# The convolution's bias goes into X ahead of time, and relu and sum become one VectorE operation

## The chip, the cores and the metric

The kernel runs on one core of a Trainium2 chip. The metric is the time of one execution on the device, in microseconds (us). The engines are named as in the profile: PE is TensorE (PEld its weight loads), ACT is ScalarE, DVE is VectorE, POOL is GpSimd, SP issues the DMAs.

## What is computed

For 32 images of 64 channels and 32 x 32 positions: a group norm, a convolution block, an attention block and a layer of eight experts with a residual around each. Only the first block matters here.

```python
def _L0_conv_ref(x, info_w, info_b, mask_w, mask_b, out_w, out_b):
    info = relu(einsum('ic,bchw->bihw', info_w, x) + info_b)
    mask = sigmoid(einsum('mc,bchw->bmhw', mask_w, x) + mask_b)
    expanded = (mask[:, :, None] * info[:, None]).reshape(B, MC * IC, H, W)
    return relu(einsum('oe,behw->bohw', out_w, expanded) + out_b)
...
x = x + _L0_conv_ref(_gn(x), ...)
t = tokens(x)
t = t + attention(_ln_t(t), ...)
t = t + experts(_ln_t(t), ...)
```

Everything is in float32. Since relu(z + b) = max(z, -b) + b, the sum x + relu(z + b) equals max(z, -b) + (x + b).

## The kernel before

Two images lie on the 128 partitions (a pair), with 1024 positions each. A group is two pairs (slots s = 0 and 1, `G = 2`), and there are eight groups. Each slot is worked on in two halves c of 512 columns. So a step over "pieces" is four instructions, (s, c) = (0,0), (0,1), (1,0), (1,1).

The work of a group is cut into stages with names. In one turn, group a goes through its dense stages (norm, convolution, attention) while the group before it goes through the experts: 32 units of 128x1024 hidden values, taken in 16 batches of two. A step marked H does the first layers and the Gelus of a batch (PE L794, ACT L942); a step marked Y does its second layers, the weighting and the sum (PE L809, DVE L1277, POOL L988). The table `SCHEDULE` says in which order the stages and the H and Y steps stand, the same for all engines, and each engine works through its own part of it strictly in that order. The first turn has a table of its own, `OPENING`: there group 1 (`EARLY`) is worked on beside group 0, with other buffers (XF for X, CWB for T1 and the rest, the banks HP for R).

The stages that the change touches:

- `group_norm`: DVE subtracts the mean and multiplies (L1082, 128x1024, one for each slot), from X to XN, and signals `gn_done`. Then PE multiplies XN for `info_mask_0` and `info_mask_1` (L557), ACT does relu and tanh of the result in T1 (L859, L860), and DVE splits that into two parts (L1089, L1091). `SCHEDULE` has a Y step between `group_norm` and `info_mask_0`, and an H, Y, H behind `info_mask_0`.
- `conv_out`: PE multiplies by the weights "ow" into the banks R (L587). ACT reads R, scales by 0.5, adds the bias, does relu, writes T1 and signals `oc_act` (L871). DVE adds T1 to X in place and signals `x1_done` (L1106).
- `centre_1`: PE multiplies the new X by a centering matrix into the same banks R (L642, behind `x1_done`), ACT squares (L876), DVE sums the squares (L1127). Then `rstd_1`, a chain of short DVE operations.
- `features_1` copies results of the norm to XN and XB on ACT (L884, L887), and POOL adds X to XB (L978).
- `choose_1` and `choose_2` are the DVE operations that pick two experts for each token (L1212 to L1252).
- `prepare`: some DVE operations on weights at the start, once.

Of the kernel before, what the change touches and what calls it, by code (L numbers as in the profile page):

```python
# [11 lines left out]
ALU = mybir.AluOpType  # L12
# [3 lines left out]
P = 128  # L16
# [4 lines left out]
G = 2  # L21
# [89 lines left out]
def build(nc, x, wpack, w1e, reps, out):  # L111
    xd = x.rearrange("(n two) c t -> n (two c) t", two=2)
    od = out.rearrange("(n two) c t -> n (two c) t", two=2)
    with ExitStack() as ctx:
        def sb(name, shape, dt=F32):
            return ctx.enter_context(nc.sbuf_tensor(name, shape, dt))

        def sem(name):
            return ctx.enter_context(nc.semaphore(name))

        def sems(name):
            return [sem(f"{name}{g}") for g in range(G)]
# [25 lines left out]
        W1G = sb("W1G", [P, HID])  # L148
        BH = sb("BH", [P, 1])
        BT = sb("BT", [P, 1])  # L150
        ONE = sb("ONE", [P, 2], BF16)
        MINUS = sb("MINUS", [P, 1])
        BI = sb("BI", [P, 2, 2])
# [14 lines left out]
        def w(name, rows=slice(0, P)):  # L168
            a, n = COLS[name]
            return W[rows, a:a + n]  # L170

        def col(k, rows=slice(0, P)):
            a = COLS["cols"][0] + k
            return W[rows, a:a + 1]
# [6 lines left out]
        def half(c):  # L181
            return slice(c * CH, (c + 1) * CH)
# [51 lines left out]
        ir_done = sems("ir_done")  # L234
        prod_done = sems("prod_done")
        oc_ps = sems("oc_ps")
        oc_act = sems("oc_act")
        x1_done = sems("x1_done")
        ln_ps = sems("ln_ps")
        ln_sq = sems("ln_sq")  # L240
# [60 lines left out]
        def pieces(slots):  # L301
            return [(s, c) for s in slots for c in range(NCH)]
# [4 lines left out]
        def nth(n, s, c=None):  # L307


            if c is None:  # L310
                return (n - 1) * G + s + 1
            return ((n - 1) * G + s) * NCH + c + 1

        def at(n, c):

            return (n - 1) * NCH + c + 1
# [36 lines left out]
        def slotwise(name, stage):  # L353

            return {f"{name}.{s}": (lambda s=s: stage((s,))) for s in range(G)}
# [51 lines left out]
        def convolution_buffers(a):  # L407

            if a == EARLY:
                return XF[:, 1, :, :], CWB[:, :, 0, :], CWB[:, :, 1, :], CWB[:, :, 2, :], CWB[:, :, 3:7, :], HP  # L410
            return X, XN, T1, T2, BIG, R
# [117 lines left out]
        def _(pe):  # L529
# [11 lines left out]
            def parts(a, b, par):  # L541
# [208 lines left out]
                def gates():  # L750

                    for s in range(G):
                        pe.wait_ge(xf_done[s], at(a + 1, LAST))
                        if a == 0:
                            pe.wait_ge(oc_act[s], at(EARLY + 1, LAST))
                    for part in range(2):
                        for s in range(G):
                            for h in range(2):
                                strip = 32 * (2 * s + h)
                                tokens_4 = XF[:, par, s, :].rearrange("p (q r t) -> p r q t", r=4, t=P)[:, 2 * h + part, :, :]  # L760
                                last = mm(Rg[0][strip:strip + 32, 0:T // 4], GWZ[:, 2 * E * (1 - part):2 * E * (3 - part)], tokens_4,
                                          start=(part == 0), stop=(part == 1))
                    last.then_inc(gate_ps, 1)
# [77 lines left out]
        def _(act):  # L841
# [10 lines left out]
            def parts(a, b, par):  # L852
                Xa, XNa, T1a, T2a, BIGa, Ra = convolution_buffers(a)

                def info_mask(s):

                    act.wait_ge(im_ps, nth(a + 1, s))
                    info, mask = img(s), img(1 - s)
                    f(T1a[info, s, 0:CH], Ra[s][info, 0:CH], ACT.Relu, bias=BI[info, 0, 0:1])  # L859
                    f(T1a[mask, s, 0:CH], Ra[s][mask, 0:CH], ACT.Tanh, bias=BT[mask, :], scale=0.5).then_inc(im_act, 1)  # L860

# [2 lines left out]
                        act.wait_ge(rep_ps[s], at(a * NREP + 3 * k + 1, c))  # L864
                        f(T2a[:, s, half(c)], Ra[s][:, half(c)], ACT.Copy).then_inc(ir_done[s], 1)

                def conv_out(slots):

                    for s, c in pieces(slots):
                        act.wait_ge(oc_ps[s], at(a + 1, c))  # L870
                        f(T1a[:, s, half(c)], Ra[s][:, half(c)], ACT.Relu, bias=col(B_OUT), scale=0.5).then_inc(oc_act[s], 1)  # L871

                def square(k, slots):
                    for s, c in pieces(slots):
                        act.wait_ge(ln_ps[s], at(a * LNS + k, c))
                        f(T2[:, s, half(c)], R[s][:, half(c)], ACT.Square).then_inc(ln_sq[s], 1)  # L876
# [23 lines left out]
                def copy_out(ready, n, dst, done, slots):  # L900
                    for s, c in pieces(slots):
                        act.wait_ge(ready[s], at(n, c))
                        f(dst[:, s, half(c)], R[s][:, half(c)], ACT.Copy).then_inc(done[s], 1)

                def exponential(n, slots):
                    for s, c in pieces(slots):
# [38 lines left out]
                def expert(step, m):  # L945
# [1 line left out]
                        gelus(m)  # L947

                return {
                    "info_mask_0": lambda: info_mask(0), "info_mask_1": lambda: info_mask(1),  # L950
                    **slotwise("info_0", lambda slots: info(0, slots)), **slotwise("info_1", lambda slots: info(1, slots)),
                    **slotwise("conv_out", conv_out), **slotwise("centre_1", lambda slots: square(1, slots)),
                    **slotwise("features_1", features_1), **slotwise("query", lambda slots: exponential(1, slots)),
                    **slotwise("key", lambda slots: exponential(2, slots)), **slotwise("kv_turn", kv_turn),
                    **slotwise("numerator", numerator), **slotwise("message", lambda slots: square(2, slots)),
# [43 lines left out]
        def _(dve):  # L999
# [3 lines left out]
            def prepare():  # L1003

                dve.wait_ge(w_rest, 16)
                v.tensor_scalar(W1G[:, :], w("w1"), col(G1), None, ALU.mult).then_inc(dve_prep, 1)
                dve.wait_ge(prep_pe, 1)
                v.tensor_copy(WMC[:, :], YP[0][:, 0:P]).then_inc(dve_prep, 1)
                v.tensor_copy(W2C[:, :], YP[0][:, P:P + C]).then_inc(dve_prep, 1)
                v.tensor_copy(BH[:, :], YP[0][:, P + C:P + C + 1]).then_inc(dve_prep, 1)  # L1010
                v.memset(GWZ[:, :], 0.0).then_inc(dve_prep, 1)
                dve.wait_ge(dve_prep, 5)
                dve.wait_ge(pads_set, 1)
                v.tensor_copy(GWZ[:, 2 * E:4 * E], w("gw")).then_inc(dve_prep, 1)
                dve.wait_ge(dve_prep, 6)
                v.memset(ST[:, 0, 30:31], 0.0).then_inc(prep_done, 1)

            def parts(a, b, par):
# [66 lines left out]
                def info_mask(s):  # L1085

                    dve.wait_ge(im_act, nth(a + 1, s))
                    high = IM[:, s, 0, :]
                    v.tensor_copy(high, T1a[:, s, 0:CH]).then_inc(hl_high, 1)  # L1089
                    dve.wait_ge(hl_high, nth(a + 1, s))  # L1090
                    v.tensor_tensor(IM[:, s, 1, :], T1a[:, s, 0:CH], high.bitcast(F32), ALU.subtract).then_inc(hl_done, 1)  # L1091
# [10 lines left out]

                def conv_out(slots):
                    for s, c in pieces(slots):
                        dve.wait_ge(oc_act[s], at(a + 1, c))
                        v.tensor_tensor(Xa[:, s, half(c)], Xa[:, s, half(c)], T1a[:, s, half(c)], ALU.add)\  # L1106
                            .then_inc(x1_done[s], 1)
                        if c == LAST and a != EARLY:
                            set_ones(s)
# [277 lines left out]
```

## Time and profile before

| what | value |
|---|---|
| median of 3 runs | 1195.16 us (1192.1 to 1196.35) |
| the profiled execution, its own time | 1201.06 us |
| its span in the trace | 1199.2 us |
| PE busy | 1075.0 us, 90% |
| DVE busy | 783.8 us, 65% |
| ACT busy | 681.4 us, 57% |
| POOL busy | 359.3 us, 30% |

The profile is of one execution. The chain that ended last, followed back from the last instruction, lies for 68% of the span on PE, 16% on DVE and 12% on ACT. A steady turn takes about 141 us, and it repeats nearly to the hundredth of a microsecond: L1082 starts at 542.22 us in one turn, and the ACT operation behind it (L859) at 262.38, 403.30, 544.22, 685.14, 826.06 and 967.01 us in the six turns that have it. All numbers of one place are therefore given for the turn around 542 us. A figure such as "x2 2.12" is the time from the start of the first of two instructions to the end of the second.

### The profile page before, as it was taken

How to read it: one execution, taken by the hardware profiler on the slowest of the kernel's cores; microseconds unless marked ns; L12 is line 12 of the kernel's file. 1: busy time of each engine (PE TensorE's matmuls, PEld its weight loads, DVE VectorE, ACT ScalarE, POOL GpSimd, SP SyncE). 2: the span in 40 equal slices, each digit the busy share in tenths (PEclk: the TensorE clock that was granted, in tenths of full speed). 3: DMA queues.
4: the chain of work that ended last, by engine and by line, in shares of the span. 5: the costliest groups of instructions: out<-in, count | busy, mean ns of one | idle time of the engine just before them, and what ended most of it. 6: DMA issues, size and time to landing. Idle time of an engine off the chain costs nothing.

```text
span 1199.2 us, 15483 instructions
## 1 busy us (share of the span) xinstructions
PE 1075.0 (90%) x5863; PEld 497.3 (41%) x5878; DVE 783.8 (65%) x1673; ACT 681.4 (57%) x930; POOL 359.3 (30%) x277
## 2 busy tenths in 40 slices
PE   5888759989999899998999989998999989999898
PEld 2454526433554245442453424542354424534232
DVE  4764746588556975488655886659754887547434
ACT  2336345755755656665657656565566555676454
POOL 0100031244312433134322344123431342314465
PEclk9987889999999999999999999999999999999999
DMA  4010069006810095102940059100771019400580
GB/s 148 1 36 1 1 145 211 1 18 132 207 36 18 1 210 129 34 18 53 223 98 1 18 119 219 36 15 4 166 173 36 19 29 222 88 1 18 113 198 27
DMA packets 17418, 96.64 MB, mean 81 GB/s; under 512 B 3648, under 2 KB 6720, under 8 KB 13120
## 3 DMA queue, kind: packets, MB, share of 16 engines
q1 hardware_dynamic: 17344, 95.66, 34.5%
q8 instruction: 46, 0.75, 0.3%
q14 instruction: 28, 0.23, 0.1%
HBM read 77.82 MB, written 9.44 MB: 73 GB/s over the span
## 4 chain that ended last, share of the span: by engine, by line
PE 68%; DVE 16%; ACT 12%; issue 3%; SPq 1%; DMA 0%; DVEq 0%; POOL 0%; POOLq 0%; ACTq 0%
PE HP L809 14%; PE HP L794 12%; PE R L642 7%; PE R L729 5%; ACT H L942 5%; PE R L598 5%; PE R L587 4%; PE R L578 3%; DVE SM L1127 3%; PE R L660 3%; PE R L651 2%; PE R L736 2%; PE R L809 2%; DVE TM L1277 2%; ACT XB L887 1%
## 5 line engine op out<-in xcount | busy, mean ns | idle before, releaser
L988 POOL TENSOR_TENSOR XB<-TM,XB 128x512 f32<-128x512 f32 x254 | 321.3, 1287 | 670.4 <-DVE TM L1277 670.3
L942 ACT ACTIVATE H<-HP,W 128x1024 f32<-128x1024 f32 x224 | 237.6, 1113 | 112.3 <-PE HP L794 111.8
L794 PE MATMUL HP<-XF,W1E 64*128 64x512 f32 x1024 | 256.0, 618 | 24.3 <-DVE TM L1277 23.8
L1277 DVE SCALAR_TENSOR_TENSOR TM<-HP,B2S,CWB 128x512 f32<-128x512 f32 x224 | 161.5, 746 | 132.4 <-PE HP L809 129.1
L809 PE MATMUL HP<-H,W 128*64 128x512 f32 x896 | 226.4, 613 | 22.1 <-ACT H L942 22.1
L794 PEld LDWEIGHTS HP<-XF,W1E 64*128 64x128 f32 x1024 | 87.3, 185 | 148.1 <-DVE TM L1277 82.2
L876 ACT ACTIVATE T<-R 128x512 f32<-128x512 f32 x128 | 73.8, 598 | 101.5 <-PE R L642 89.0
L809 PEld LDWEIGHTS HP<-H,W 128*64 128x64 f32 x896 | 49.4, 135 | 170.6 <-ACT H L942 132.5
L1127 DVE TENSOR_REDUCE SM<-T 128x8 f32<-128x512 f32 x128 | 85.1, 684 | 29.5 <-ACT T L876 27.3
L1099 DVE SCALAR_TENSOR_TENSOR BIG<-R,T 128x512 f32<-128x512 f32 x112 | 70.2, 685 | 30.1 <-PE R L578 29.8
L598 PE MATMUL R<-W,T 128*128 128x128 f32 x512 | 73.4, 289 | 5.7 <-DVE T L1146 5.2
L1154 DVE SCALAR_TENSOR_TENSOR BIG<-T,R 128x512 f32<-128x512 f32 x64 | 41.8, 684 | 49.7 <-ACT T L908 49.7
L598 PEld LDWEIGHTS R<-W,T 128*128 128x128 f32 x512 | 56.8, 145 | 40.5 <-DVE T L1146 33.7
L729 PE MATMUL R<-BIG,W1G 128*128 128x512 f32 x128 | 64.5, 633 | 2.2 <-ACT BIG L894 0.5
L1146 DVE TENSOR_TENSOR T<-R,SM 128x512 f32<-128x512 f32 x96 | 59.6, 683 | 0.6
L908 ACT ACTIVATE T<-R,MINUS 128x512 f32<-128x512 f32 x64 | 41.4, 687 | 19.7 <-PE R L651 19.6
L587 PE MATMUL R<-BIG,W 128*64 128x512 f32 x224 | 52.6, 623 | 0.0
L578 PE MATMUL R<-IM,REP 32*128 32x512 f32 x336 | 49.4, 475 | 2.9 <-DVE IM L1091 1.6
L978 POOL TENSOR_TENSOR XB<-XB,X 128x1024 f32<-128x1024 f32 x14 | 32.9, 2354 | 61.3 <-ACT XB L887 61.3
L871 ACT ACTIVATE T<-R,W 128x512 f32<-128x512 f32 x28 | 19.2, 687 | 53.8 <-PE R L587 53.8
L1277 DVE SCALAR_TENSOR_TENSOR TM<-R,B2S,CWB 128x512 f32<-128x512 f32 x32 | 23.9, 751 | 37.9 <-PE R L809 32.0
L942 ACT ACTIVATE BIG<-HP,W 128x1024 f32<-128x1024 f32 x32 | 33.9, 1110 | 26.0 <-PE HP L794 26.0
(165 smaller groups left out, 1363.9 us busy)
## 6 DMA issues: line engine op xcount, KB each, us to landing
CWB<-gates_hbm SPq DMA_DIRECT2D x32, 1536.0 KB, 22.0
CWB<-gates_hbm SPq DMA_DIRECT2D x32, 512.0 KB, 10.0
BIG<-XN SPq DMA_DIRECT2D x32, 256.0 KB, 4.5
out<-XB SPq DMA_DIRECT2D x15, 512.0 KB, 2.9
X<-x SPq DMA_DIRECT2D x14, 512.0 KB, 7.8
W<-wpack SPq DMA_DIRECT2D x1, 1064.0 KB, 5.0
XF<-x SPq DMA_DIRECT2D x2, 512.0 KB, 6.2
gates_hbm<-CWR SPq DMA_DIRECT2D x16, 64.0 KB, 1.6
```

The source lines that it names most:

```text
L578: last = mm(Ra[s][:, half(c)], REP[rows, n, :], IM[rows, s, part, :], start=(part == 0), stop=(part == 1))
L587: last = mm(Ra[s][img(k), half(c)], w("ow")[:, C * h:C * h + C], BIGa[:, s, 2 * k + h, half(c)], start=(h == 0), stop=(h == 1))
L598: last = nc.tensor.transpose(R[s][:, P * j:P * j + P], src[:, s, P * j:P * j + P], w("ident"))
L642: last = mm(R[s][:, P * j:P * j + P], src[:, s, P * j:P * j + P], weights, start=True, stop=True)
L729: mm(R[s][:, half(c)], W1G[:, :], U[s][k][:, half(c)], start=True, stop=True)\
L794: last = mm(HP[u % BATCH][:, half(k)], W1E[img(k), e, :], XF[img(k), 1 - par, s, half(c)], start=True, stop=True)
L809: last = mm(sums_of(b, u)[img(k), :], w("w2e")[:, C * e:C * e + C], activated(b, u)[:, k, :], start=True, stop=True)
L876: f(T2[:, s, half(c)], R[s][:, half(c)], ACT.Square).then_inc(ln_sq[s], 1)
L942: f(activated(b, u).rearrange("p k t -> p (k t)"), HP[u % BATCH][:, :], ACT.Gelu, bias=col(B1E + e))\
L988: nc.gpsimd.tensor_tensor(acc, TM[:, u % BATCH, :], acc, ALU.add).then_inc(acc_done, 1)
L1127: v.reduce_sum(SM[:, 0, s, some_norms(c)], norms(T2[:, s, half(c)]), AX_X).then_inc(ln_stat[s], 1)
L1277: v.scalar_tensor_tensor(out=TM[:, u % BATCH, :], in0=sums_of(b, u), scalar=B2S[:, e % 2, e // 2:e // 2 + 1], in1=CWB[:, s, e, half(c)], o ...
```

## The change

- ACT no longer does relu at `conv_out`. Instead it has a stage at `group_norm`: once `gn_done` of a slot is there, it adds the bias to X in place, one instruction of 128x1024 for each slot, and signals `xb_set`.
- DVE's operation at `conv_out` reads the bank R itself: the larger of R and -bias, plus X, into X. It waits for `oc_ps` (PE) and `xb_set` in place of `oc_act`.
- `prepare` scales the weights "ow" by 0.5 in place and writes -bias to LEAST: two more DVE operations, once.
- PE waits at the gates of group 0 for `x1_done` of group 1, no longer for `oc_act`.

```diff
-                            pe.wait_ge(oc_act[s], at(EARLY + 1, LAST))
+                            pe.wait_ge(x1_done[s], at(EARLY + 1, LAST))
...
-                def conv_out(slots):
-
-                    for s, c in pieces(slots):
-                        act.wait_ge(oc_ps[s], at(a + 1, c))
-                        f(T1a[:, s, half(c)], Ra[s][:, half(c)], ACT.Relu, bias=col(B_OUT), scale=0.5).then_inc(oc_act[s], 1)
...
+                def with_bias():
+
+                    for s in range(G):
+                        act.wait_ge(gn_done, nth(a + 1, s))
+                        source = convolution_buffers(a)[0]
+                        f(source[:, s, :], source[:, s, :], ACT.Identity, bias=col(B_OUT)).then_inc(xb_set, 1)
...
+                    "group_norm": with_bias, "info_mask_0": lambda: info_mask(0), "info_mask_1": lambda: info_mask(1),
...
+                v.tensor_scalar(w("ow"), w("ow"), 0.5, None, ALU.mult).then_inc(dve_prep, 1)
+                v.tensor_scalar(LEAST[:, :], col(B_OUT), -1.0, None, ALU.mult).then_inc(dve_prep, 1)
...
                 def conv_out(slots):
                     for s, c in pieces(slots):
-                        dve.wait_ge(oc_act[s], at(a + 1, c))
-                        v.tensor_tensor(Xa[:, s, half(c)], Xa[:, s, half(c)], T1a[:, s, half(c)], ALU.add)\
+                        dve.wait_ge(oc_ps[s], at(a + 1, c))
+                        if c == 0:
+                            dve.wait_ge(xb_set, nth(a + 1, s))
+                        v.scalar_tensor_tensor(out=Xa[:, s, half(c)], in0=Ra[s][:, half(c)], scalar=LEAST[:, :], in1=Xa[:, s, half(c)],
+                                               op0=ALU.max, op1=ALU.add)\
                             .then_inc(x1_done[s], 1)
```

ACT in a steady turn, from the exponential of the gates to `info_mask_1`, before (line numbers of the kernel before):

```order
L934 ACTIVATE RT<-RT 128x2x128 [waits lg_shifted]
L942 ACT_TABLE_LOAD
L942 ACTIVATE H<-HP,W 128x1024 [waits l1_ps] x2
L859 ACTIVATE T<-R,BI 64x512 [waits im_ps]
L860 ACTIVATE T<-R,BT 64x512
L942 ACTIVATE H<-HP,W 128x1024 [waits l1_ps] x4
```

And the same place in the changed kernel (its line numbers are up to a few higher or lower; L944 is the Gelu, L860 and L861 are relu and tanh of `info_mask`):

```order
L936 ACTIVATE RT<-RT 128x2x128 [waits lg_shifted]
L944 ACT_TABLE_LOAD
L944 ACTIVATE H<-HP,W 128x1024 [waits l1_ps] x2
L905 ACTIVATE X<-X,W 128x1024 [waits gn_done] x2
L860 ACTIVATE T<-R,BI 64x512 [waits im_ps]
L861 ACTIVATE T<-R,BT 64x512
L944 ACTIVATE H<-HP,W 128x1024 [waits l1_ps] x4
```

The two new operations (L905) stand between two batches of Gelus, ahead of `info_mask_0`; no load of a table is added there.

DVE in a steady turn at `conv_out`, before:

```order
L1099 SCALAR_TENSOR_TENSOR BIG<-R,T 128x512 [waits rep_ps1] x2
L1106 TENSOR_TENSOR X<-X,T 128x512 [waits oc_act0] x2
L1112 MEMSET BIG 128x8x2
L1106 TENSOR_TENSOR X<-X,T 128x512 [waits oc_act1] x2
L1112 MEMSET BIG 128x8x2
L1127 TENSOR_REDUCE SM<-T 128x8 [waits ln_sq0] x2
```

And now:

```order
L1103 SCALAR_TENSOR_TENSOR BIG<-R,T 128x512 [waits rep_ps1] x2
L1112 SCALAR_TENSOR_TENSOR X<-R,LEAST,X 128x512 [waits xb_set,oc_ps0]
L1112 SCALAR_TENSOR_TENSOR X<-R,LEAST,X 128x512 [waits oc_ps0]
L1119 MEMSET BIG 128x8x2
L1112 SCALAR_TENSOR_TENSOR X<-R,LEAST,X 128x512 [waits xb_set,oc_ps1]
L1112 SCALAR_TENSOR_TENSOR X<-R,LEAST,X 128x512 [waits oc_ps1]
L1119 MEMSET BIG 128x8x2
L1134 TENSOR_REDUCE SM<-T 128x8 [waits ln_sq0] x2
```

The number and the place of the operations stay; what they read and what they wait for is different.

ACT in the first turn, where group 1 is normalized beside group 0, before:

```order
L884 ACTIVATE XN<-R 128x512 [waits ln_back0]
L887 ACTIVATE XB<-R,W 128x512
L859 ACTIVATE CWB<-HP,BI 64x512 [waits im_ps]
L860 ACTIVATE CWB<-HP,BT 64x512
L859 ACTIVATE CWB<-HP,BI 64x512 [waits im_ps]
L860 ACTIVATE CWB<-HP,BT 64x512
L908 ACTIVATE T<-R,MINUS 128x512 [waits qk_ps1] x2
```

And now:

```order
L879 ACTIVATE XN<-R 128x512 [waits ln_back0]
L882 ACTIVATE XB<-R,W 128x512
L905 ACTIVATE XF<-XF,W 128x1024 [waits gn_done] x2
L860 ACTIVATE CWB<-HP,BI 64x512 [waits im_ps]
L861 ACTIVATE CWB<-HP,BT 64x512
L860 ACTIVATE CWB<-HP,BI 64x512 [waits im_ps]
L861 ACTIVATE CWB<-HP,BT 64x512
L910 ACTIVATE T<-R,MINUS 128x512 [waits qk_ps1] x2
```

Both new operations on XF come between the last copy of `features_1` and the first relu of `info_mask_0` of group 1.

## Rows read from the trace of the kernel before

**Rows 1.** The page, section 4: the chain that ended last, by engine.
```profile
PE 68%; DVE 16%; ACT 12%; issue 3%; SPq 1%; DMA 0%; DVEq 0%; POOL 0%; POOLq 0%; ACTq 0%
```

**Rows 2.** Groups by shape: busy us, mean ns of one | idle before, releaser.
```profile
L871 ACT ACTIVATE T<-R,W 128x512 f32<-128x512 f32 x28 | 19.2, 687 | 53.8 <-PE R L587 53.8
...
L1106 DVE TENSOR_TENSOR X<-X,T 128x512 f32<-128x512 f32 x28 | 22.5, 804 | 18.5 <-ACT T L871 18.0
...
L1200 DVE SCALAR_TENSOR_TENSOR XB<-R,W,XB 128x512 f32<-128x512 f32 x32 | 21.8, 745 | 0.0
...
L876 ACT ACTIVATE T<-R 128x512 f32<-128x512 f32 x128 | 73.8, 598 | 101.5 <-PE R L642 89.0
...
L942 ACT ACTIVATE H<-HP,W 128x1024 f32<-128x1024 f32 x224 | 237.6, 1113 | 112.3 <-PE HP L794 111.8
```

**Rows 3.** The line of ACT's one large copy from SBUF: duration min/median/max ns.
```profile
L845 ACT ACTIVATE REP<-BIG x1: 842/842/842, 9.9 to 9.9; 128x768 fp32r<-128x768 f32 x1
```

**Rows 4.** Chain from conv_out to centre_1: start us, us, what.
```profile
578.64 7.02 PE R L587 x32
585.67 3.78 PE R L642 x32
...
589.47 0.61 ACT T L876
```

**Rows 5.** Timeline of conv_out: start us, us, instruction [idle before, releaser].
```profile
579.43 2.51 POOL L988 TENSOR_TENSOR XB<-TM,XB 128x512 f32<-128x512 f32 x2 [4.41 <-DVE TM L1277]
...
581.28 1.21 DVE L1106 TENSOR_TENSOR X<-X,T 128x512 f32<-128x512 f32 x1
...
586.43 0.69 DVE L1106 TENSOR_TENSOR X<-X,T 128x512 f32<-128x512 f32 x1 [1.02 <-ACT T L871]
586.79 0.60 ACT L876 ACTIVATE T<-R 128x512 f32<-128x512 f32 x1 [0.39 <-PE R L642]
```

**Rows 6.** Timeline of a steady turn, group_norm to choose_2, as in rows 5.
```profile
542.22 1.54 DVE L1082 TENSOR_SCALAR XN<-X,R,SG 128x1024 f32<-128x1024 f32 x2
...
544.22 0.68 ACT L859 ACTIVATE T<-R,BI 64x512 f32<-64x512 f32 x1 [2.60 <-PE R L557]
...
545.65 2.12 ACT L942 ACTIVATE H<-HP,W 128x1024 f32<-128x1024 f32 x2
...
546.82 2.08 PE L809 MATMUL HP<-H,W 128*64 128x512 f32 x8 [0.35 <-ACT H L942]
...
547.96 0.43 DVE L1089 CAST IM<-T 128x512 fp32r<-128x512 f32 x1
...
549.03 1.40 DVE L1277 SCALAR_TENSOR_TENSOR TM<-HP,B2S,CWB 128x512 f32<-128x512 f32 x2
...
549.85 2.68 POOL L988 TENSOR_TENSOR XB<-TM,XB 128x512 f32<-128x512 f32 x2 [2.67 <-DVE TM L1277]
550.35 0.41 DVE L1219 TENSOR_REDUCE RT<-RT 128x32 f32<-128x256 f32 x1
...
550.79 0.62 DVE L1220 TENSOR_TENSOR RT<-RT 128x256 f32<-128x256 f32 x1
...
551.44 1.38 DVE L1212 SCALAR_TENSOR_TENSOR RT<-RT,W 128x256 f32<-128x256 f32 x1
```

**Rows 7.** Timeline of the first turn, group 1 beside group 0, as in rows 5.
```profile
56.24 4.71 POOL L978 TENSOR_TENSOR XB<-XB,X 128x1024 f32<-128x1024 f32 x2 [54.97 <-ACT XB L887]
...
58.13 0.69 ACT L859 ACTIVATE CWB<-HP,BI 64x512 f32<-64x512 f32 x1
...
59.55 1.69 DVE L1089 CAST IM<-CWB 128x512 fp32r<-128x512 f32 x1 [3.13 <-ACT CWB L860]
60.11 0.68 ACT L860 ACTIVATE CWB<-HP,BT 64x512 f32<-64x512 f32 x1
...
61.89 0.42 DVE L1089 CAST IM<-CWB 128x512 fp32r<-128x512 f32 x1
...
62.95 2.48 DVE L1154 SCALAR_TENSOR_TENSOR BIG<-T,R 128x512 f32<-128x512 f32 x4
```

More of the change, by code:

```diff
@@ L150, in build @@
         BT = sb("BT", [P, 1])
+        LEAST = sb("LEAST", [P, 1])
         ONE = sb("ONE", [P, 2], BF16)
@@ L236, in build @@
         oc_ps = sems("oc_ps")
-        oc_act = sems("oc_act")
+        xb_set = sem("xb_set")
         x1_done = sems("x1_done")
@@ L949, in parts @@
                 return {
-                    "info_mask_0": lambda: info_mask(0), "info_mask_1": lambda: info_mask(1),
+                    "group_norm": with_bias, "info_mask_0": lambda: info_mask(0), "info_mask_1": lambda: info_mask(1),
                     **slotwise("info_0", lambda slots: info(0, slots)), **slotwise("info_1", lambda slots: info(1, slots)),
-                    **slotwise("conv_out", conv_out), **slotwise("centre_1", lambda slots: square(1, slots)),
+                    **slotwise("centre_1", lambda slots: square(1, slots)),
                     **slotwise("features_1", features_1), **slotwise("query", lambda slots: exponential(1, slots)),
@@ L1010, in prepare @@
                 v.tensor_copy(BH[:, :], YP[0][:, P + C:P + C + 1]).then_inc(dve_prep, 1)
+                v.tensor_scalar(w("ow"), w("ow"), 0.5, None, ALU.mult).then_inc(dve_prep, 1)
+                v.tensor_scalar(LEAST[:, :], col(B_OUT), -1.0, None, ALU.mult).then_inc(dve_prep, 1)
                 v.memset(GWZ[:, :], 0.0).then_inc(dve_prep, 1)
-                dve.wait_ge(dve_prep, 5)
+                dve.wait_ge(dve_prep, 7)
                 dve.wait_ge(pads_set, 1)
                 v.tensor_copy(GWZ[:, 2 * E:4 * E], w("gw")).then_inc(dve_prep, 1)
-                dve.wait_ge(dve_prep, 6)
+                dve.wait_ge(dve_prep, 8)
                 v.memset(ST[:, 0, 30:31], 0.0).then_inc(prep_done, 1)
```

## The prediction, made before the changed kernel ran

> **What bounds the kernel now.** I read four views. First the chain that ended last, by engine [rows 1]: PE carries 68% of it, so an operation of ACT or DVE counts only where PE or the chain stands waiting for it. Then the groups by shape, for prices [rows 2, 3]. Then the chain and the timeline where an operation goes away [rows 4, 5]. Last, the timelines of the two places where one is added [rows 6, 7].
>
> The reader should see in [rows 4] that at `conv_out` and `centre_1` the chain never leaves PE: 7.02 us of L587, then 3.78 us of L642 with no gap, and only then ACT. ACT's relu and DVE's sum run beside that. ACT's total idle time ahead of L871, 53.8 us, is time in which it waits for PE, and DVE's ahead of L1106, 18.0 us, is time in which it waits for ACT [rows 2]; neither is time in which PE waits.
>
> **What is removed.** 32 relus (4 pieces in 8 groups; 28 of them have the shape of [rows 2], 4 are those of group 1) of 687 ns: 22.0 us of ACT's work, and a latency of 0.69 us between PE and DVE. What of it lies on the path? The last piece is the tightest. Its sum on DVE starts at 586.43 and ends at 587.12 [rows 5]. PE needs it for the last quarter of L642, which runs from 585.67 for 3.78 us [rows 4], so that quarter begins at 585.67 + 2.84 = 588.5. The slack is 1.4 us before the change and 2.1 us after. For the first piece it is larger, since PE still has three pieces of `conv_out` to do. ACT's squares start behind PE, too (0.39 us idle, released by L642 [rows 5]). So the removal is worth **0**. The cover is PE's 10.8 us without a gap; if it were gone, each group would gain up to 0.69 us.
>
> DVE's operation itself changes its price. Before it took 804 ns on the average, 0.69 us in the plain case and 1.21 us where it met POOL [rows 2, 5]. The new one reads a bank, a scalar from SBUF and one tile of SBUF, which is the form of L1200: 745 ns. So it is 0.06 us dearer in the plain case, and 0.5 us cheaper for the first piece of a group, if it does not wait for POOL. Both lie in the cover of PE named above, except in group 1, where two such operations stand twice among DVE's work that PE waits for: 4 x 0.06 = 0.24 us at most, which I take into the upper bound and not into the sum.
>
> On that first piece a page bears. L1106 started at 581.28 and ended at 582.49, 0.55 us behind the end of POOL's pair at 581.94 [rows 5]. The Trainium skill says (SBUF — State Buffer, Who interferes with whom) that a DVE instruction with two inputs in SBUF and a GpSimd instruction that reads SBUF shut each other out for a whole instruction, while DVE with one input in SBUF is free of it. The trace agrees with the first half. By that rule the changed DVE operation never waits for POOL, and DVE has 0.5 us a turn more; it would be worth time only as rival C below.
>
> **What is added at group_norm.** 16 operations of ACT, 128x1024, with bias, from SBUF to SBUF. No row has this form. From 512 to 1024 columns an operation with bias grows from 687 to 1113 ns, 0.832 ns a column, and the bias costs 687 - 598 = 89 ns [rows 2]. The copy from SBUF with 768 columns takes 842 ns [rows 3], so 842 - 639 = 203 ns are fixed. That gives 852 + 203 + 89 = 1.14 us. Two in a row overlap: two Gelus take 2.12 us [rows 6], so the second starts 2.12 - 1.11 = 1.01 us behind the first, 0.10 less than its duration. I count a pitch of 1.04 us, with 1.14 as the upper end and 1.01 as the lower. The sum is 16 x 1.14 = 18.2 us of work for the 22.0 that go, so ACT's total falls a little; the place is what matters.
>
> The Trainium skill gives ScalarE about 93 ns of access overhead on SBUF against about 51 on PSUM (Perfetto Trace Analysis, Optimizing Scalar/DVE Operations). By it the operation would cost about 40 ns more than one from a bank; rows 2 and 3 give 203 - (598 - 426) = 31 ns. The sum does not change by it.
>
> Queued behind the two on ACT are relu and tanh of `info_mask_0` and the next two Gelus, and for these PE waits (L809, released by ACT), and for PE then DVE. In the steady turn [rows 6]: the first L1082 of the pair ends half-way, at about 543.03. The additions start at 543.07 and 544.11, and relu can start at 545.15, where it started at 544.22 before. From relu to Gelu it was 545.65 - 544.22 = 1.43, so the Gelus start at 546.58: **0.93 us late** (0.87 to 1.14). PE's L809 slides by the same.
>
> Does it reach the end? DVE is the bound here. It comes to L1277 at 549.03, and with 1.40 us for two it starts the second at about 549.70. The second result of L809 came at 546.82 + 2.08 = 548.90; with the delay it comes at 549.83, so the second L1277 starts at 549.88, **0.18 us late** (0.1 to 0.4). The first has slack (its result came 1.04 us earlier). Behind it come L1219, L1220 and L1212, and these do not run freely: L1220 took 0.62 and L1212 1.38 us, where L1219, of the same width, took 0.41. L1220 ends at 551.41, so with 0.42 of work it began at about 550.99, when POOL had the first of its pair behind it (549.85 + half of 2.68, less a little), and L1212 ends at 552.82, 0.29 behind POOL's pair (552.53). Both wait for POOL, and a lateness of 0.18 us disappears in these waits: L1220 is there at 550.97 in place of 550.79 and still goes at 550.99. So a steady turn loses **0** (0 to 0.4), six times.
>
> **What is added in the first turn.** For group 0 the additions fall into the start of the program, where nothing else is queued on ACT, and PE still waits for weights from memory. The two operations of `prepare` (128x128 and 128x1) are shorter than L1219 with its 0.41 us [rows 6] and stand where DVE, too, is early. I count 0 for both, with 2 x 0.41 = 0.8 us as the upper end. For group 1 there is no such room [rows 7]: L859 follows the copies at once, at 58.13, and now 2 x 1.04 = 2.08 us later. DVE waits for its results (3.13 us idle before L1089), so all of it seems to pass. But L1089 at 59.55 took 1.69 us where its twin took 0.42: it ended at 61.24, 0.29 behind POOL's pair (56.24 + 4.71 = 60.95). Now its input comes at about 61.6, POOL is done, and it takes 0.42. The second tanh ended at 60.11 + 0.68 = 60.79 and now at 62.87. The second L1089 thus starts at 62.89 in place of 61.89, and L1154, on which PE waits, at 63.95 in place of 62.95: **1.0 us late** (0 if DVE's later waits swallow it, 2.1 if POOL's work moves too).
>
> **The sum**, against the profiled execution: 1201.06 + 0 + 6 x 0 + 1.0 = 1202.1 us. That execution is 5.9 us above the median of the runs, so the same +1.0 on the median gives **1196.2 us**.
>
> **The rivals.**
>
> A, slower: the lateness of the Gelus goes through whole. DVE's lead of 0.8 us at L1277 and its waits for POOL are what stops it; if DVE were not the bound there (for instance since POOL's pair ends earlier than its record, so that L1220 and L1212 wait for something else), a turn would lose 0.93 us. Six turns and the first: 5.6 + 1.0 = +6.6, 1201.8 us. It decides at the second L1277: without DVE's lead there, all of the delay counts, with it only what is beyond 0.8 us. For it: the Gelu stands in the chain here. Against: DVE has no idle time in [rows 6] from 549.03 to 552.82.
>
> B, the order at POOL turns round: L1220 comes 0.02 us before POOL's first operation is over, which is close. If POOL's second gets in ahead of it, L1220 waits to about 552.3, ends at 552.7, and L1212 at 553.1 in place of 552.82: 0.3 us in six turns, +1.8, with the first turn +2.8, 1198.0 us. The Trainium skill has a rule for it (SBUF — State Buffer, Who interferes with whom): the one that issues first holds the shared ports for its whole instruction, and the other is shut out.
>
> C, faster by DVE's freed time: 7 groups x 0.5 us of waits for POOL that vanish, if DVE and not PE led at `conv_out`: 1.0 - 3.5 = -2.5, 1192.7 us. Against it: [rows 4].
>
> D, faster by the shorter way: 0.69 us in each of 8 groups, if the sums were late for L642: 1.0 - 5.5 = -4.5, 1190.7 us. Against it: the slack of 1.4 us.
>
> E, the change does not do what it says: the addition could need far more than 1.14 us on its unshown form, or DVE's operation could. With a pitch of 1.4 us the Gelus come 1.65 us and the second L1277 0.9 us late, and the case becomes A.
>
> **How the numbers follow.** My forecast 0.60, B 0.13, A with E 0.14, C 0.07, D 0.06. About 0.3%, 3.6 us, is what a measurement of this kernel can tell from no change. Forecast, B and C lie inside it: same 0.80. A and E give slower 0.14, D gives faster 0.06. The range holds forecast and B with the upper bounds (1.0 + 0.24 + 6 x 0.4 = +3.6, and a little for the spread of the runs, whose median can fall a microsecond or two to either side) and the lower bound with C in part: 1193.0 to 1200.0. A and D stay outside, 0.20.
>
> **What would show it.** In the changed profile: `conv_out` and `centre_1` still 7.02 and 3.78 us of PE without a gap; additions of 1.14 us at a pitch of about 1.04; the Gelus behind `info_mask_0` 0.9 us later against L1082; the stretch from L1082 to the L1212 of `choose_2` unchanged within 0.1 us; L1154 in the first turn 1.0 us later. A turn longer than now by 0.3 us speaks for B, by 0.9 for A; a shorter one for C or D. The forecast is wrong if the pair of additions takes over 2.8 us, or if PE has idle time at `centre_1` that the records hide.

## The result, and the profile after

| kernel | median | runs | span of its profiled execution |
|---|---|---|---|
| before | 1195.12 us (1192.08 to 1196.6) | 20 | 1199.2 us |
| changed | 1197.66 us (1196.0 to 1201.31) | 20 | 1194.1 us |

The ratio is 1.0027, with a 95% interval of 1.0017 to 1.0037: 3.2 us slower (2.0 to 4.4), where +1.0 was forecast. The profiled execution of the changed kernel is nevertheless 5 us shorter than that of the kernel before: executions of one kernel differ by more than the change is worth. So the two spans can't be subtracted; the two traces have to be compared place by place.

**conv_out.** The chain of the changed kernel, and then its timeline (start us, us, instruction [idle before, releaser]), at the place of [rows 4] and [rows 5]:

```profile
571.88 7.02 PE R L588 x32
578.90 3.78 PE R L643 x32
582.68 0.02 issue
582.71 0.61 ACT T L871
```

```profile
572.66 2.52 POOL L990 TENSOR_TENSOR XB<-TM,XB 128x512 f32<-128x512 f32 x2 [4.42 <-DVE TM L1284]
...
574.36 0.74 DVE L1112 SCALAR_TENSOR_TENSOR X<-R,LEAST,X 128x512 f32<-128x512 f32 x1
575.52 0.75 DVE L1112 SCALAR_TENSOR_TENSOR X<-R,LEAST,X 128x512 f32<-128x512 f32 x1 [0.42 <-PE R L588]
...
580.03 0.60 ACT L871 ACTIVATE T<-R 128x512 f32<-128x512 f32 x1 [10.04 <-PE R L643]
```

PE takes 7.02 and 3.78 us, to the hundredth what it took before. ACT, which had 0.39 us of idle time ahead of its first square, has 10.04 now, and the square still comes when PE has the data. That is the picture of work taken off an engine on which nobody waited. The first DVE operation runs beside POOL's pair and takes 0.74 us, where it took 1.21.

The groups by shape (busy us, mean ns of one | idle before, releaser) give the prices of the two new forms:

```profile
L1112 DVE SCALAR_TENSOR_TENSOR X<-R,LEAST,X 128x512 f32<-128x512 f32 x28 | 20.9, 747 | 15.2 <-PE R L588 15.2
...
L905 ACT ACTIVATE X<-X,W 128x1024 f32<-128x1024 f32 x14 | 15.3, 1141 | 9.0 <-DVE XN L1086 9.0
```

**group_norm.** The timeline of the steady turn, at the place of [rows 6]:

```profile
535.38 1.55 DVE L1086 TENSOR_SCALAR XN<-X,R,SG 128x1024 f32<-128x1024 f32 x2
536.24 2.19 ACT L905 ACTIVATE X<-X,W 128x1024 f32<-128x1024 f32 x2 [1.45 <-DVE XN L1086]
...
538.33 0.67 ACT L860 ACTIVATE T<-R,BI 64x512 f32<-64x512 f32 x1
...
539.71 2.12 ACT L944 ACTIVATE H<-HP,W 128x1024 f32<-128x1024 f32 x2
...
542.20 1.65 DVE L1284 SCALAR_TENSOR_TENSOR TM<-HP,B2S,CWB 128x512 f32<-128x512 f32 x2
...
543.02 2.73 POOL L990 TENSOR_TENSOR XB<-TM,XB 128x512 f32<-128x512 f32 x2 [2.67 <-DVE TM L1284]
543.76 0.41 DVE L1226 TENSOR_REDUCE RT<-RT 128x32 f32<-128x256 f32 x1
...
544.20 0.42 DVE L1227 TENSOR_TENSOR RT<-RT 128x256 f32<-128x256 f32 x1
544.66 1.38 DVE L1219 SCALAR_TENSOR_TENSOR RT<-RT,W 128x256 f32<-128x256 f32 x1
```

Counted from the start of the norm, the Gelus come after 4.33 us (3.43 before): 0.90 late. The pair of L1284 takes 1.65 us in place of 1.40: its second half waits 0.25 us. Then look at L1227. Before, the same operation was there 8.57 us behind the norm and took 0.62, since it waited for POOL's first sum; now it is there after 8.82 and takes 0.42. Its end moved by only 0.05 us, from 9.19 to 9.24. The wait for POOL has swallowed the rest. In both kernels L1219 (L1212 before) takes 1.38 us and ends 0.29 us behind POOL's pair, and that pair ends 10.37 us behind the norm, where it ended after 10.31. So the steady turn is 0.06 us late at this place.

**The first turn**, at the place of [rows 7]:

```profile
57.41 0.74 ACT L882 ACTIVATE XB<-R,W 128x512 f32<-128x512 f32 x1
...
57.98 2.24 ACT L905 ACTIVATE XF<-XF,W 128x1024 f32<-128x1024 f32 x2
...
61.48 0.43 DVE L1093 CAST IM<-CWB 128x512 fp32r<-128x512 f32 x1 [5.66 <-ACT CWB L861]
...
62.75 0.43 DVE L1093 CAST IM<-CWB 128x512 fp32r<-128x512 f32 x1
...
63.82 2.47 DVE L1161 SCALAR_TENSOR_TENSOR BIG<-T,R 128x512 f32<-128x512 f32 x4
```

The cast that took 1.69 us beside POOL takes 0.43 now. From the last copy of `features_1` to L1161 it is 63.82 - 57.41 = 6.41 us. In the kernel before it was 62.95 - 57.56 = 5.39, by [rows 7] and the row of its last copy:

```profile
57.56 0.73 ACT L887 ACTIVATE XB<-R,W 128x512 f32<-128x512 f32 x1
```

So L1161 comes 1.02 us late. For group 0 the first cast comes 4.34 us behind the norm, where it came after 4.29: the additions of group 0 cost 0.05 us there.

**All profiles side by side.** Where the rest of the difference comes from shows only over many executions. The columns: time from the norm of group 1 to that of group 2; a steady turn (norm to norm, the usual value of five); from the norm of group 7 to the end; and the time for which the granted clock was 0.5 of full speed between 40 and 170 us, summed up from the trace's record of the clock.

| profile | group 1 to 2 | steady turn | group 7 to end | half speed |
|---|---|---|---|---|
| before | 205.49 | 140.92 | 234.23 | 44 |
| before, second | 201.28 | 140.93 | 234.28 | 34 |
| before, third | 198.29 | 140.90 | 234.24 | 27 |
| changed | 199.13 | 140.98 | 235.59 | 27 |
| changed, second | 199.23 | 141.00 | 235.64 | 27 |
| changed, third | 204.33 | 140.97 | 234.29 | 34 |

Two things are to be read here. The steady turn repeats to 0.03 us, and the change costs 0.07 us of it (one turn of the five takes 0.15 us more; see the last section). The stretch between group 1 and 2 does not repeat: it differs by 7 us between executions of the kernel before, and within each kernel it is longer where the clock stood at the lower of its two levels (1.2 in place of 2.4 GHz) for longer.

The third profile of the kernel before and the first of the changed one have the same 27 us at half speed. Between them the stretch from group 1 to 2 differs by 0.84 us, five steady turns together by 0.55 and the end by 1.35. The clock fell at the same places in these two, so this pair shows what the change costs by its own length. The other pair with equal time at half speed (34 us, the second profile of before and the third of the changed) differs by 3.05 us from group 1 to 2. There the clock fell at other places, and the time at half speed alone does not tell what it costs.

### The profile page after: what moved, and what is told of

Same layout as the page of the kernel before. It is cut to its first block, busy times and chain, and to the rows that moved or that the text cites. A ratio compares the mean times of both kernels' runs of the same rounds, so it can differ in the third digit from the quotient of the medians.

```text
span 1194.1 us, 15484 instructions
## 1 busy us (share of the span) xinstructions
PE 1067.6 (89%) x5863; PEld 493.0 (41%) x5878; DVE 780.0 (65%) x1675; ACT 675.5 (57%) x914; POOL 359.7 (30%) x277
## 4 chain that ended last, share of the span: by engine, by line
PE 64%; DVE 17%; ACT 14%; issue 3%; SPq 1%; DMA 0%; DVEq 0%; POOL 0%; POOLq 0%; ACTq 0%
PE HP L810 13%; PE HP L795 11%; PE R L643 7%; PE R L730 5%; ACT H L944 5%; PE R L599 5%; PE R L588 4%; PE R L579 3%; DVE SM L1134 3%; PE R L661 3%; PE R L652 2%; PE R L737 2%; PE R L810 2%; DVE TM L1284 2%; ACT XB L882 1%
## 5 line engine op out<-in xcount | busy, mean ns | idle before, releaser
L944 ACT ACTIVATE H<-HP,W 128x1024 f32<-128x1024 f32 x224 | 237.6, 1113 | 108.4 <-PE HP L795 108.1
L1284 DVE SCALAR_TENSOR_TENSOR TM<-HP,B2S,CWB 128x512 f32<-128x512 f32 x224 | 161.9, 746 | 133.9 <-PE HP L810 130.5
L1161 DVE SCALAR_TENSOR_TENSOR BIG<-T,R 128x512 f32<-128x512 f32 x64 | 41.8, 683 | 49.7 <-ACT T L910 49.7
L1284 DVE SCALAR_TENSOR_TENSOR TM<-R,B2S,CWB 128x512 f32<-128x512 f32 x32 | 23.9, 750 | 37.9 <-PE R L810 32.5
L944 ACT ACTIVATE BIG<-HP,W 128x1024 f32<-128x1024 f32 x32 | 33.9, 1110 | 26.0 <-PE HP L795 26.0
L926 ACT ACTIVATE BIG<-R,BH 128x512 f32<-128x512 f32 x64 | 40.4, 689 | 5.1 <-PE R L730 4.9
```

Of the source, the lines that this page charges most:

```text
L944: f(activated(b, u).rearrange("p k t -> p (k t)"), HP[u % BATCH][:, :], ACT.Gelu, bias=col(B1E + e))\
L1284: v.scalar_tensor_tensor(out=TM[:, u % BATCH, :], in0=sums_of(b, u), scalar=B2S[:, e % 2, e // 2:e // 2 + 1], in1=CWB[:, s, e, half(c)], o ...
```

## The experiments

### Both places, one at a time

The first group has the changed kernel as its yardstick, and three kernels that move the additions of ACT (L905) to places where ACT was idle. Nothing else differs.

```diff
-                    "group_norm": with_bias,
+                    ("low_0.1" if a == EARLY else "group_norm"): with_bias,
...
+                    ("group_norm" if starting(a) or a == EARLY else "high_1.0"): with_bias,
...
+                    ("low_0.1" if a == EARLY else "group_norm" if starting(a) else "high_1.0"): with_bias,
```

The first new line is `m1_first_turn_moved`, the second `m2_steady_moved`, the third `m3_both_moved`.

> The changed kernel itself, as the yardstick of this group. Theory 1 (the two additions of group 1 in the first turn cost 1.0 us, each of the six steady turns 0.06 us, and what is left of the measured +3.2 us comes from TensorE's clock, which falls to half speed in other stretches of the first 170 us): +1.4 us that the trace accounts for, +2.5 to +3.5 us in the median against the kernel before. Rival theory (a cost in the steady turns that the profile does not show): the same median, so this run alone decides nothing.

Measured: 1.0018 (1.0001 to 1.0036) against the kernel before, median 1196.59 us. That is 2.2 us (0.1 to 4.3) by the ratio and 1.6 by the medians of this group: less than the 2.5 to 3.5 us that were expected, though the interval holds them.

> Only the additions of group 1 are moved, to a place in the first turn where ACT was idle for 6.24 us (before L919 of the kernel before). Theory 1: L1161 in the first turn comes 1.0 us earlier against the last copy of features_1 than in the changed kernel, and the time falls by 1.0 us plus what the clock gave in addition, so to within 0.5 us of the kernel before, some +0.4 us. Rival theory (steady turns): it falls by nothing or by 1.0 us at most and stays 2 us above the kernel before.

Measured: 1.0009 (0.9991 to 1.0026), median 1197.11 us; the mean of its 12 runs is 1196.2, that of all 42 runs of the changed kernel 1197.6 and that of the 112 runs of the kernel before 1194.4. What was expected of the place is met: in its timeline the additions (last row, of ACT) stand in ACT's pause, and the cast is back at 1.68 us beside POOL:

```profile
59.50 1.68 DVE L1093 CAST IM<-CWB 128x512 fp32r<-128x512 f32 x1 [3.54 <-ACT CWB L861]
61.82 0.42 DVE L1093 CAST IM<-CWB 128x512 fp32r<-128x512 f32 x1
62.88 2.47 DVE L1161 SCALAR_TENSOR_TENSOR BIG<-T,R 128x512 f32<-128x512 f32 x4
...
77.39 2.19 ACT L905 ACTIVATE XF<-XF,W 128x1024 f32<-128x1024 f32 x2
```

From the last copy (57.51) to L1161 it is 5.37 us, so the 1.0 us is gone. The time fell by 1.4 us in the mean, and to +1.8 against the kernel before, not to the +0.4 that was expected; with 12 runs that scatter over 4 us the two can't be told apart.

> Only the additions of the six steady turns are moved, from group_norm to high_1.0, where ACT was idle for 3.8 us ahead of the relus that are gone. The additions of groups 0 and 1 stay. Theory 1: the Gelus behind info_mask_0 are back where they were, 3.43 us behind L1086, a turn falls from 140.98 to 140.92 us, and the time by 0.3 to 0.4 us, so +2.2 to +3.1 us against the kernel before. Rival theory: it falls by 2 us or more.

Measured: 1.0022 (1.0004 to 1.0040), median 1197.62 us, mean 1197.6. The steady turns are back at 140.92 to 140.95, but for the one that is 0.15 us longer, and the time in all is that of the changed kernel. By the turns the rival (2 us in the steady turns) falls. The time alone, a difference of 0.0 us in the mean with some 1.7 to either side, excludes it only just.

> Both moves together. Theory 1: no addition is on the path any more, the removal of the relus was worth 0, so the time is that of the kernel before within 0.5 us. If the removal had been worth something that the additions hid (the prediction's cases C and D), it shows here: 2 to 5 us below the kernel before.

Measured: 0.9994 (0.9979 to 1.0009), median 1193.32 us. The additions now stand behind the last Gelus ahead of `conv_out`, and nothing waits for them:

```profile
565.93 2.12 ACT L944 ACTIVATE H<-HP,W 128x1024 f32<-128x1024 f32 x2 [0.46 <-PE HP L795]
567.95 2.18 ACT L905 ACTIVATE X<-X,W 128x1024 f32<-128x1024 f32 x2
578.10 0.60 ACT L871 ACTIVATE T<-R 128x512 f32<-128x512 f32 x1 [7.97 <-PE R L643]
```

It was run once more for a narrower interval:

> The kernel with both additions moved, once more, since its ratio of 0.9994 (0.9979 to 1.0009) leaves open whether it beats the kernel before. Theory 1 (nothing of the change on the path): within 0.5 us of the kernel before. If the removal of the relus has a value that the first interval hid: 1 us or more below it.

Measured: 1.0006 (0.9989 to 1.0022), median 1195.09 us. Both groups together, 24 runs, have a mean of 1194.8 us against the 1194.4 of the kernel before. So with the additions at these places the change is worth nothing, to within about 1 us to either side, and no version here is shown to beat the kernel before.

### The two halves of the change apart

`m4_no_addition` leaves the bias out: no stage with additions on ACT, and no wait for `xb_set`. `m5_addition_alone` is the kernel before with the additions.

The first, against the changed kernel:

```diff
-                    "group_norm": with_bias,
...
-                        if c == 0:
-                            dve.wait_ge(xb_set, nth(a + 1, s))
```

The second, against the kernel before:

```diff
+                    "group_norm": with_bias,
...
                         dve.wait_ge(oc_act[s], at(a + 1, c))
+                        if c == 0:
+                            dve.wait_ge(xb_set, nth(a + 1, s))
```

> The kernel before once more, for a second profile of it, since its first profiled execution (1201.06 us) lies above the median of its runs. Theory 1 (the time between executions of one kernel differs only by where TensorE's clock falls to half speed in the first 170 us and near 1120 us): the six steady turns take 140.92 us again, to 0.02, and all of the difference to the first profile lies between the norms of group 1 and group 2 (205.5 us there) and behind the norm of group 7 (234.2 us). Rival: the steady turns differ as well.

Measured: median 1194.81 us; steady turns of 140.92 to 140.93, and the rest as in the table above. The difference of 4.8 us in span between this profile and the first lies for 4.2 us between the norms of group 1 and 2. The rest was expected behind the norm of group 7 and is not there (234.28 against 234.23): the norm of group 1 starts 0.68 us earlier.

> The removal alone: the changed kernel without the 16 additions, so the bias of the convolution is left out of the sum (the result is x + max(z, -b)). Theory 1 (the removal is worth nothing): steady turns of 140.92 us, L588 and L643 still 7.02 and 3.78 us without a gap, and the time of the kernel with both additions moved, 0 to 1 us off the kernel before. Rival (the relus' way or DVE's waits for POOL cost time): turns of 140.2 us (0.69 less) or 140.4 (0.5 less), and 3 to 5 us less in all.

Measured: 1.0008 (0.9996 to 1.0019), median 1194.15 us, mean 1194.5. Steady turns of 140.93 us (the five: 140.93, 140.95, 140.93, 140.92, 140.95). The chain, at conv_out:

```profile
574.13 7.02 PE R L588 x32
581.15 3.78 PE R L643 x32
```

The removal alone is worth nothing. The prediction's cases C and D (0.5 or 0.69 us a group) are excluded: the steady turns, which repeat to 0.03 us, would have shown either.

> The additions alone: the kernel before, with the 16 additions at group_norm, and the relus and sums as they were, so the bias of the convolution is in the sum twice. Theory 1: it pays what the changed kernel pays, turns of 141.00 us (0.08 each) and L1154 of the first turn 1.0 us later against the last copy of features_1, so +2 to +4 us. Rival: the change's cost comes from what DVE does at conv_out in its new form, and this kernel has the time of the kernel before within 1 us.

Measured: 1.0045 (1.0029 to 1.0061), median 1198.48 us in 6 runs. Steady turns of 140.95 to 140.99, L1154 6.40 us behind the last copy (5.39 before). That is 5.4 us by the ratio (3.5 to 7.3), above the +2 to +4 that were expected; with 6 runs the excess may be scatter. The addition alone pays at least all that the changed kernel pays (3.2 us, 2.0 to 4.4), so the cost is that of the additions, and nothing points to a cost of DVE's new form. Its last stretch took 234.3 us, not 235.6.

### How much delay is swallowed

These two kernels lengthen ACT's wait in the steady turns by one more addition (for slot 0) and by two (one for each slot), into a scratch tile, so that the result stays.

```diff
                         source = convolution_buffers(a)[0]
+                        if not (starting(a) or a == EARLY):
+                            f(T2[:, s, :], source[:, s, :], ACT.Identity, bias=col(B_OUT))
                         f(source[:, s, :], source[:, s, :], ACT.Identity, bias=col(B_OUT)).then_inc(xb_set, 1)
```

That is `m6_doubled`; `m7_one_more` has `s == 0 and` in the condition.

> The changed kernel with a second addition for each slot in the six steady turns, ahead of the true one and into the scratch tile T2; the result is the same. It doubles the wait of the Gelus. Theory 1 (a delay of 0.9 us is swallowed by DVE's lead of 0.8 us and its waits for POOL, and nothing beyond): the Gelus come 3.1 us late in place of 0.9 and the first and second L1284 behind them 1.9 and 2.3 us late; none of that is swallowed any more, so a turn takes 141.00 + 2.2 = 143.2 us and the whole +13 us against the changed kernel. Rival (a delay costs its proportion, 0.08 us for 0.9): a turn of 141.2 us, +1 us in all.

> The changed kernel with one more addition, for slot 0 only, in each of the six steady turns (into the scratch tile T2; the result is the same): the Gelus come 2.0 us late, between the 0.9 of the changed kernel and the 3.1 of the doubled one. Theory 1 (all beyond DVE's lead of 0.8 us and what POOL's turn hides is paid one for one): the second L1284 behind the Gelus 1.25 us late and a turn of 141.00 + 1.1 = 142.1 us, so +6.5 us against the changed kernel. Rival (the doubled kernel paid for a second thing, such as the late L1095 of DVE): 141.3 us a turn, +2 us.

Measured: 1.0192 (1.0173 to 1.0210) and 1.0116 (1.0088 to 1.0143), so +23 and +14 us against the kernel before, where +16 and +9 were expected with the 2.5 to 3 us of the changed kernel. The steady turns tell why. The turns of the doubled kernel took 143.83, 144.27, 144.32, 143.18 and 143.17 us, those with one more 142.10, 143.50, 143.69, 143.64 and 142.13. The lowest of each are the 143.2 and 142.1 that were expected, to 0.03. The others have something in addition. The timeline of the kernel with one more, in one of its turns (norm at 830.40):

```profile
832.31 2.18 ACT L907 ACTIVATE X<-X,W 128x1024 f32<-128x1024 f32 x2
834.39 0.67 ACT L860 ACTIVATE T<-R,BI 64x512 f32<-64x512 f32 x1
835.07 0.68 ACT L861 ACTIVATE T<-R,BT 64x512 f32<-64x512 f32 x1
835.77 2.12 ACT L946 ACTIVATE H<-HP,W 128x1024 f32<-128x1024 f32 x2
...
838.15 0.75 DVE L1286 SCALAR_TENSOR_TENSOR TM<-HP,B2S,CWB 128x512 f32<-128x512 f32 x1 [0.85 <-PE HP L810]
839.15 0.75 DVE L1286 SCALAR_TENSOR_TENSOR TM<-HP,B2S,CWB 128x512 f32<-128x512 f32 x1 [0.25 <-PE HP L810]
```

The Gelus are 1.94 us late (5.37 us behind the norm, 3.43 before), and DVE, which had no idle time here, now waits 0.85 us for PE; the second L1286 is 1.27 us late, where 1.25 was expected. A delay of 0.9 us costs a turn 0.07, one of 1.9 costs 1.2 and one of 3.0 costs 2.25. From the second point to the third that is one for one.

What comes on top is the clock. Two stretches of the kernel with one more, in a turn of 142.10 and in one of 143.50 us, at the same distance behind their norms (columns: stretch, length, then busy us of PE, PEld, DVE, ACT, POOL, granted clock, DMA share, GB/s):

```profile
269.90:273.90 4.00, 2.12 (x16) 0.46 (x12) 3.83 (x12) 1.36 (x2) 0.55 (x1) 1.00 0.00 0
273.90:277.90 4.00, 4.00 (x22) 1.20 (x22) 3.74 (x7) 2.12 (x2) 2.31 (x3) 1.00 0.01 2
```

```profile
412.00:416.00 4.00, 2.11 (x16) 0.46 (x12) 3.83 (x12) 1.36 (x2) 0.54 (x1) 1.00 0.00 0
416.00:420.00 4.00, 4.00 (x14) 1.27 (x12) 3.13 (x5) 2.23 (x2) 2.13 (x2) 0.57 0.00 0
```

The first line of each pair is the same in both turns: PE works for 2.1 of 4 us, DVE for all of it. Behind it the clock stays at full speed in one turn and is 0.57 in the mean in the other, where 14 matmuls of PE lie in the 4 us in place of 22. Three of the five turns had this, and it cost each 1.4 to 1.6 us; in the doubled kernel it was three of five, too, for 0.65 to 1.15 us each. In the kernel before and in the changed one no steady turn has it, in three profiles of each. In the four stretches of 4 us that begin 0.43 us behind the norm, PE is busy for 12.08 us of 16 before, 12.06 in the changed kernel, 10.96 with one more addition and 10.40 with two (in a turn without a fall). So the longer pauses of PE go with the falls, but they don't decide them: with one more addition, turns with the same sum went both ways.

### The last stretch

> The changed kernel once more, for a third profile. In both so far the stretch behind the norm of group 7 took 235.6 us, with a half-speed stretch of 6.83 us near 1120 us, where all other kernels had 3.41 us and 234.1 to 234.4 us. Theory 1 (where the clock falls depends on where PE's pauses happen to lie in time, and not on the additions, since the kernel with the additions alone had 3.41 us there): either value can come. Rival (the change itself brings it): 6.83 us and 235.6 us again. Steady turns of 141.00 us by both.

Measured: 1.0023 (1.0010 to 1.0036), median 1197.56 us. The stretch behind the norm of group 7 took 234.29 us this time. In the first profile of the changed kernel the clock was low for twice as long there (columns as above):

```profile
1104.00:1112.00 8.00, 4.88 (x18) 1.45 (x20) 7.44 (x16) 2.12 (x2) 3.18 (x3) 0.91 0.00 0
1112.00:1120.00 8.00, 7.93 (x26) 2.25 (x22) 1.99 (x4) 2.60 (x3) 3.31 (x4) 0.67 0.13 33
```

And in the third:

```profile
1104.00:1112.00 8.00, 7.54 (x30) 1.80 (x28) 7.17 (x11) 4.21 (x4) 5.17 (x4) 1.00 0.00 0
1112.00:1120.00 8.00, 5.11 (x18) 1.69 (x18) 4.60 (x13) 1.93 (x3) 2.49 (x2) 0.80 0.00 0
```

A mean clock of 0.91 and 0.67 over 8 us each makes 2 x (0.09 + 0.33) x 8 = 6.7 us at half speed, 0.80 makes 3.2. The third execution is 4.8 us later at this point, so the rows give the time at half speed and not the same work. The rival falls as it stands: the change does not bring the 1.35 us in every execution. Whether it brings them more often is open. Two of three profiles of the changed kernel have the longer end and none of the three of the kernel before; and 14 of the 42 runs of the changed kernel have the mean clock of those two executions (0.985) and about their time (1196.05 and 1196.49 us; the 14 took 1195.85 to 1196.7).

> A third profile of the kernel before. Theory 1: steady turns of 140.92 us once more; the stretch from the norm of group 1 to that of group 2 somewhere between 197 and 206 us, by the time that the clock stands at half speed in it.

Measured: 1192.68 us in the one run; steady turns of 140.90 to 140.93 and 198.29 us between the norms of group 1 and 2.

## Why the prediction was right, and where it was too small

- **What bounds the kernel, and the removal at 0.** Right, and shown by the kernel without additions. The cover named was PE's 10.8 us without a gap, and it is there in the six steady turns of every profile.
- **The price of the addition.** 1.14 us were put together from a slope and two fixed costs; the row says 1141 ns. The pair took 2.19 us (1.14 + 1.04 was expected). The Trainium skill gives an ACTIVATE whose bias is a pointer operand of 128x1 about 280 ns + 0.833 ns for each column (ScalarE: Activation LUTs, What ACT_TABLE_LOAD costs), an estimate of 1133 ns here; the trace agrees within 8 ns. DVE's new form took 747 ns (745 expected), and the first of a turn took 0.74 us beside POOL's pair, where the old form took 1.21. The Trainium skill says that a DVE instruction with at most one input in SBUF, outside the modes that use two ports, does not contend with GpSimd (SBUF — State Buffer, Who interferes with whom); the trace agrees with these 0.74 us.
- **The steady turn at 0.** The delay of the Gelus was 0.90 (0.93 expected), the second L1284 was 0.25 late (0.18 expected). The term that was mis-sized is the last step, "a lateness of 0.18 us disappears": of 0.25 us all but 0.05 to 0.07 vanished in the wait for POOL. Six times that is 0.4 us; the five turns measured make 0.55, with the one that takes 0.15 more. Case B, the turned order at POOL, did not come: L1227 took 0.42 us ahead of L1219's 1.38, so it still went between POOL's two sums. Case A's price without DVE's lead was measured by the two lengthened kernels: beyond about 0.8 us each microsecond of delay costs one.
- **The first turn at +1.0.** 1.02 late in its timeline, and the cast beside POOL shrank from 1.69 to 0.43 us as the step had it. In the pair of profiles with the clock's falls at the same places, 0.84 us of it reached the norm of group 2. The additions of group 0, put at 0, cost 0.05 us at the first cast.
- **What the sum left out.** 1.0 + 0.4 = 1.4 us are shown by place. The measured difference is 3.2 us (2.0 to 4.4), so more than half of it stands in no term. The range held it, but by its width: the upper end was made of 0.4 us in each steady turn, which did not come, and of the spread of the runs. The remainder could be missed because the prediction treats the time of the first turn as fixed. It is not: the clock stands at half speed there for 27 to 44 us, and one stretch of one kernel takes 198 to 205 us. Moving both additions brought 2.8 us back in the mean (1197.6 to 1194.8, give or take 1 us), and the kernel with the additions alone pays it all. So it is shown that the additions at their place cost more than their own length of 1.4 us, probably about twice as much.
- **Whether the clock is the remainder.** This is not shown. The mean granted clock of the runs gives it little room: 0.9842 in the 92 runs of the kernel before that have it on record, 0.9837 in the 42 of the changed kernel. These 0.0005 of 1195 us are 0.6 us of full speed lost, give or take 0.9. If the clock is the cause, then rather by where it falls than by how long it is low. Which of the two places brings the remainder stays open, too: the means with one place moved, 1196.2 and 1197.6, rest on 12 runs each that scatter over 4 and 7 us. The longer end may be a part of it: 14 runs of 42 with 1.35 us more would be 0.45 us in the mean (an estimate).

One thing makes the clock plausible without showing it: a pause of PE grew in the first turn. Ahead of L625 PE sat idle for 3.47, 3.39 and 3.62 us in the three profiles of the changed kernel, and ahead of the same operation for 1.80, 2.47 and 2.61 us in those of the kernel before. The third profile of the kernel before, and then the third of the changed one:

```profile
63.01 0.39 PE L624 MATMUL R<-ONE 128*128 128x512 bf16 x1 [2.61 <-DVE BIG L1154]
```

```profile
64.30 0.39 PE L625 MATMUL R<-ONE 128*128 128x512 bf16 x1 [3.62 <-DVE BIG L1161]
64.52 1.05 PE L652 MATMUL R<-W,XN 128*128 128x128 f32 x8
65.41 0.58 PE L625 MATMUL R<-ONE 128*128 128x512 bf16 x1
65.79 1.91 PE L652 MATMUL R<-W,XN 128*128 128x128 f32 x8
```

Right behind the longer pause the clock fell: the same eight matmuls take 1.05 us and then 1.91. No profile of the kernel before has a fall at this place, and this is the profile whose stretch from group 1 to 2 is 3.05 us longer at equal time at half speed. But the first two profiles of the changed kernel have the long pause without the fall, and one with the additions moved (the second run of `m3_both_moved`) has a fall there behind a pause of 2.18 us. The lengthened kernels show that such a thing can act: with PE's wait about 1 us longer than in the changed kernel, three steady turns in five had a stretch at half speed.

The Trainium skill says that the clock gate runs on a schedule of its own, which does not start anew with a kernel (TensorE: Matmul & The Clock Gate, Part 1). The traces agree so far as that equal turns of one execution got different clocks. That this schedule is why executions of one kernel differ, and that a change can shift the shares of them, no run here shows.

## What to carry to other kernels

Work moved off an engine is worth only what somebody waits for: look for the engine's idle time ahead of the work (here ACT waited for PE) and whether the bounding engine has a gap behind it (here none, over 10.8 us). The new place of the work decides the sign: in a queue that is worked off in order, put it behind the last thing that somebody waits for and not ahead of it, even if the engine looks idle there; the same additions cost about 3 us at `group_norm` and nothing that 24 runs can show where ACT waited for PE with nothing queued behind it. A delay that is smaller than the lead of the engine behind it is nearly free (0.9 us cost 0.07), and beyond it each microsecond costs one (1.9 cost 1.2, 3.0 cost 2.25). A longer pause of PE can also bring a stretch at half the clock, 0.65 to 1.6 us a turn in the two lengthened kernels. And where executions of one kernel differ by more than the change is worth, compare traces place by place, take several profiles of each kernel, and don't pick one pair.

## What was not expected of the hardware

- Equal turns of one execution, with equal busy times of all engines up to the place, got a granted clock of 1.00 in two turns and about 0.57 over 4 us in three, for 1.4 to 1.6 us each.
- Waits for POOL repaid a delay: an operation of DVE that came 0.25 us later took 0.20 less, and a cast that came 2.08 us later (4.07 us behind the last copy of `features_1` in place of 1.99) took 1.26 less.
- One of the five steady turns takes 0.15 us more in all three profiles of the changed kernel (141.11 to 141.14, beside 140.99) and in the four of the kernels with moved additions (141.08 to 141.17). It does not in the kernel before, nor in those with only one half of the change. In it one L1284 comes 0.34 to 0.38 us late, against another turn of the same profile, with no engine late ahead of it. The cause stays open.
